# Summing a tile's scaled parts: a DMA that adds and one reduce, in place of GpSimd's adds and four VectorE adds

## The reference, cut to what matters

```
e = stack([tbl_0[ids[:, 0]], ..., tbl_39[ids[:, 39]]], axis=1)      # 512 x 40 x 16
x = x0 = e
for k in (k0, k1, k2):                                              # each 128 x H x 40
    x = einsum('bhd,bmd,ohm->bod', x, x0, k)
    outputs.append(sum(x, axis=-1))
z = concatenate(outputs, axis=1)                                    # 512 x 384
h = relu(concatenate([z, dense_ctx], 1) @ W_top1 + b_top1)
y = relu(h @ W_top2 + b_top2) @ W_top3
```

## Time and profile before

| | |
|---|---|
| median of 3 runs | 821.02 us |
| the profiled execution: span, first to last instruction | 817.8 us (the fastest of the three runs took 817.72) |
| TensorE busy | 690.5 us (84%) |
| VectorE busy | 668.2 us (82%) |
| ScalarE busy | 523.9 us (64%) |
| GpSimd busy | 499.1 us (61%) |
| mean granted TensorE clock | 0.971 |
| DMA moved | 43.07 MB, mean 53 GB/s |

### The profile page before, as it was taken

One profiled execution on the slowest core, in us unless ns is written; L12 is line 12 of the kernel. 1 busy time (PEld: TensorE's weight loads), 2 busy tenths in 40 slices (PEclk: granted clock), 3 DMA queues, 4 the chain that ended last, 5 costly groups with the idle time before them and its releaser, 6 DMA issues.

```text
span 817.8 us, 12851 instructions
## 1 busy us (share of the span) xinstructions
PE 690.5 (84%) x2558; PEld 477.1 (58%) x2558; DVE 668.2 (82%) x1542; ACT 523.9 (64%) x1753; POOL 499.1 (61%) x443
## 2 busy tenths in 40 slices
PE   0157988899898979797988898988979797998998
PEld 0126666566565757575655666665657575775384
DVE  2325989898988989898979898989979797989191
ACT  2205676676775767676666776767757676788193
POOL 6304767767667777685867767776767783564000
PEclk9998999999999999999999999999999998998599
DMA  6261111111212121212111111112121211010000
GB/s 187 63 171 61 44 55 53 45 64 38 70 25 76 22 77 25 76 31 69 35 60 46 49 58 45 62 37 70 19 77 22 75 30 64 36 42 26 0 1 1
DMA packets 45543, 43.07 MB, mean 53 GB/s; under 512 B 25615, under 2 KB 28943, under 8 KB 45216
## 3 DMA queue, kind: packets, MB, share of 16 engines
q1 hardware_dynamic: 40352, 41.07, 15.3%
q0 software_dynamic: 5120, 1.32, 2.2%
HBM read 41.06 MB, written 1.97 MB: 53 GB/s over the span
## 4 chain that ended last, share of the span: by engine, by line
DMA 37%; PE 21%; POOL 15%; issue 10%; SPq 7%; DVE 7%; ACT 2%; DVEq 1%; POOLq 0%; ACTq 0%
DMA pairs<-scratch 24%; POOL fold L350 7%; POOL x0g L309 7%; DMA scratch<-x0g 5%; DMA x0g<-in_table,rows_now 4%; DMA scratch<-scratch 4%; PE Y L622 4%; PE Y L624 3%; PE Y L623 3%; DVE chain L534 3%; SPq L268 3%; SPq L278 2%; DVE chain L497 2%; SPq L273 1%; DVE pairs L462 1%
## 5 line engine op out<-in xcount | busy, mean ns | idle before, releaser
L417 ACT ACTIVATE scaled<-Y,xtok 128x128 f32<-128x128 f32 x1536 | 422.7, 380 | 110.8 <-PE Y L624 100.5
L622 PE MATMUL Y<-k1lo,x1hi 128*128 128x512 f32 x640 | 296.5, 463 | 47.8 <-DVE chain L534 46.2
L624 PE MATMUL Y<-k1hi,x1lo 128*128 128x512 f32 x640 | 255.9, 400 | 0.0
L623 PE MATMUL Y<-k1hi,x1hi 128*128 128x512 f32 x640 | 255.4, 399 | 0.0
L534 DVE SCALAR_TENSOR_TENSOR chain<-Y,xtok,chain 128x128 f32<-128x128 f32 x768 | 211.6, 338 | 4.9 <-PE Y L624 4.8
L309 POOL DMA_INDIRECT x0g<-in_table,rows_now x160 | 174.5, 1091 | 42.1 <-issue 36.0
L350 POOL TENSOR_TENSOR fold<-fold,scaled 128x512 f32<-128x512 f32 x128 | 170.8, 1334 | 37.3 <-ACT scaled L417 28.3
L622 PEld LDWEIGHTS Y<-k1lo,x1hi 128*128 128x128 f32 x640 | 122.2, 191 | 118.3 <-DVE chain L534 77.6
L350 POOL TENSOR_TENSOR fold<-scaled 128x512 f32<-128x512 f32 x64 | 91.9, 1437 | 138.3 <-ACT scaled L417 111.1
L462 DVE TENSOR_TENSOR pairs<-pairs,A 120x512 f32<-120x512 f32 x112 | 96.9, 865 | 76.8 <-DMA pairs<-scratch 76.7
L623 PEld LDWEIGHTS Y<-k1hi,x1hi 128*128 128x128 f32 x640 | 122.7, 192 | 38.7 <-issue 14.4
(11 more groups left out here) (77 smaller groups left out, 453.4 us busy)
## 6 DMA issues: line engine op xcount, KB each, us to landing
pairs<-scratch SPq DMA_DIRECT2D x112, 240.0 KB
A<-scratch SPq DMA_DIRECT2D x16, 240.0 KB
k1raw<-in_k SPq DMA_DIRECT2D x1, 2560.0 KB, 10.5
x0g<-in_table,rows_now POOLq DMA_INDIRECT x160
k2s<-in_k SPq DMA_DIRECT2D x1, 2560.0 KB, 17.8
scratch<-x0g SPq DMA_DIRECT2D x64, 20.0 KB
pairs<-in_w SPq DMA_DIRECT2D x3, 256.0 KB
scratch<-scratch SPq DMA_DIRECT2D x16, 40.0 KB
```

The costliest lines, as they stand in the source:

```text
L417: ins = nc.scalar.activation(scaled[:, rank(c) - 1, i * O:(i + 1) * O], Y[(NCH * tile + c) % YB][:, i * O:(i + 1) * O], ACT.Copy, scale=xt ...
L622: nc.tensor.matmul(y, hi[:, tok], k1lo[:, cols], start=True, stop=False)
L623: nc.tensor.matmul(y, hi[:, tok], k1hi[:, cols], start=False, stop=False)
L624: nc.tensor.matmul(y, lo[:, tok], k1hi[:, cols], start=False, stop=True).then_inc(s_y, 1)
```

## The change

GpSimd's three adds a tile go. ScalarE now writes its six ranks into two buffers, each double: `sums` (four banks of 512: bank 0 is rank 1 and `chain`, banks 1, 2 and 3 are ranks 2, 3 and 6) and `more` (two banks: ranks 4 and 5). When rank 5 (chunk 6) is there, GpSimd first makes `diag`, then issues one DMA a tile that adds `more` (128 partitions x 4096 B) onto banks 1 and 2 of `sums`, and then the gathers. VectorE's four merge steps become one `tensor_reduce` over the sixteen 128-wide parts of `sums`, at c = 3 of the next tile; it waits for the DMA.

```diff
+ADDED = 2
+PARTS = NA - ADDED
-MERGE_AT = (0, 3, 3, 3)
+MERGE_AT = 3
...
                     pool.wait_ge(s_xtok, u * GPB + slot + 1)
                     pool.wait_ge(s_G, T + 1)
+                    pool.wait_ge(s_yA, NA * (T + 1) + NA - 1)
                     nc.gpsimd.tensor_tensor(diag[tile % 2][:, 0:M, :], ...)
-                    sums = fold[tile % 2]
-                    pool.wait_ge(s_merge, MERGE * T + 1)
-                    for a in range(2, NA - EXTRA):
-                        pool.wait_ge(s_yA, NA * (T + 1) + a + 1)
-                        if a > 2:
-                            pool.wait_ge(s_fold, FOLDS * (T + 1) + a - 2)
-                        nc.gpsimd.tensor_tensor(sums[:, :], scaled[:, 1, :] if a == 2 else sums[:, :],
-                                                scaled[:, a, :], ALU.add).then_inc(s_fold, 1)
+                    pool.dma_start(sums[tile % 2][:, BANK:BANK * (1 + ADDED)], more[tile % 2][:, :],
+                                   accum_op=ALU.add).then_inc(s_added[tile % 2], 16)
...
+            def place(par, r, i):
+                if r in (4, 5):
+                    return more[par][:, ((r - 4) * MB + i) * O:((r - 4) * MB + i + 1) * O]
+                k = (r - 1 if r < 4 else PARTS - 1) * MB + i
+                return sums[par][:, k * O:(k + 1) * O]
...
                             if rank(c) == 1:
-                                act.wait_ge(s_chain, STT * T + MB)
-                            elif rank(c) <= NA - EXTRA:
-                                act.wait_ge(s_fold, FOLDS * T + max(rank(c) - 2, 1))
-                            else:
-                                act.wait_ge(s_merge, MERGE * (T + 1) + rank(c) - NA + EXTRA)
+                                act.wait_ge(s_merge, T + 1)
+                            elif rank(c) == 4:
+                                act.wait_ge(s_added[tile % 2], 16 * (GPB * TPG // 2 * u + (tile + 2) // 2))
...
-            def merge(T, par, k):
-                ...
-                nc.vector.tensor_tensor(to, a, b, ALU.add).then_inc(s_merge, 1)
+            def merge(T, par, adds):
+                dve.wait_ge(s_chain, STT * (T + 2))
+                dve.wait_ge(s_added[par], 16 * adds)
+                dve.wait_ge(s_yA, NA * (T + 2))
+                nc.vector.tensor_reduce(x2[par][:, :], sums[par][:, :].rearrange("p (i o) -> p o i", o=O), AX.X,
+                                        ALU.add).then_inc(s_merge, 1)
```

More of the change, by code:

```diff
@@ L155, in build @@
         xtok = [sb(f"xtok{i}", [P, TPG, M]) for i in range(2)]
-        scaled = sb("scaled", [P, NA, BANK])
-        fold = [sb(f"fold{i}", [P, BANK]) for i in range(2)]
-        chain = [sb(f"chain{i}", [P, BANK]) for i in range(2)]
+        more = [sb(f"more{i}", [P, ADDED * BANK]) for i in range(2)]
+        sums = [sb(f"sums{i}", [P, PARTS * BANK]) for i in range(2)]
+        chain = [t[:, 0:BANK] for t in sums]
+        spot = sb("spot", [16, 8])
         x2 = [sb(f"x2_{i}", [P, O]) for i in range(2)]
@@ L183, in build @@
         w1cs, ctxs = A3[0][0:CTX, :], A3[1][0:CTX, :]
-        z2, w2s = pairs[3], over("fold0", "w2s", [P, H1 // P, H2])
-        h1 = scaled[:, 0:H1 // P, :]
+        z2, w2s = pairs[3], over("sums0", "w2s", [P, H1 // P, H2])
+        h1 = over("more0", "h1", [P, H1 // P, BANK])
         k2hi, k2lo = k1hi, k1lo
         Ghi = x1hi + pairs_hi[0:2]
-        Glo = x1lo + [pairs_hi[2], over("chain0", "Glo3", [P, B], f32r)]
+        Glo = x1lo + [pairs_hi[2], over("sums1", "Glo3", [P, B], f32r)]
         h2, ys = G[:, 0:2, 0:B], G[0:1, 2, 0:B]
@@ L217, in build @@
         s_chain = sem("chain_steps")
-        s_fold = sem("pool_folds")
+        s_added = [sem(f"added{i}") for i in range(2)]
         s_merge = sem("tile_sums_merged")
@@ L323, in _ @@
             pool.wait_ge(s_dones, 2)
-            nc.gpsimd.memset(fold[1][:, :], 0.0).then_inc(s_fold, FOLDS)
+            for i in range(2):
+                pool.dma_start(spot[:, 4 * i:4 * i + 4], ident_in[0:16, 0:4]).then_inc(s_added[i], 16)
             nc.gpsimd.memset(credit[:, 0:1], 0.0).then_inc(s_G, 1)
@@ L417, in body @@
                                 ins = nc.scalar.activation(
-                                    scaled[:, rank(c) - 1, i * O:(i + 1) * O],
+                                    place(tile % 2, rank(c), i),
                                     Y[(NCH * tile + c) % YB][:, i * O:(i + 1) * O], ACT.Copy,
@@ L478, in prep @@
                                             ALU.add).then_inc(s_x1free, 1)
-            def merge(T, par, k):
-                sums = chain[par]
-                if k == 0:
-                    dve.wait_ge(s_chain, STT * (T + 2))
-                else:
-                    dve.wait_ge(s_merge, MERGE * (T + 2) + k)
-                if k < EXTRA:
-                    dve.wait_ge(s_yA, NA * (T + 2) - EXTRA + k + 1)
-                    a, b, to = sums[:, :], scaled[:, NA - EXTRA + k, :], sums[:, :]
-                elif k == EXTRA:
-                    dve.wait_ge(s_fold, FOLDS * (T + 2))
-                    a, b, to = sums[:, :], fold[par][:, :], sums[:, :]
-                else:
-                    n = BANK >> (k - EXTRA)
-                    a, b = sums[:, 0:n], sums[:, n:2 * n]
-                    to = sums[:, 0:n] if k < MERGE - 1 else x2[par][:, :]
-                nc.vector.tensor_tensor(to, a, b, ALU.add).then_inc(s_merge, 1)
-            nc.vector.memset(chain[1][:, :], 0.0).then_inc(s_chain, STT)
-            nc.vector.memset(scaled[:, NA - EXTRA:, :], 0.0).then_inc(s_szero, 1)
-            nc.vector.memset(credit[:, 4:5], 0.0).then_inc(s_merge, MERGE)
+            def merge(T, par, adds):
[4 more added lines that the diff above has]
+                                        ALU.add).then_inc(s_merge, 1)
+            nc.vector.memset(chain[1], 0.0).then_inc(s_chain, STT)
+            nc.vector.memset(sums[1][:, BANK:], 0.0).then_inc(s_szero, 1)
+            nc.vector.memset(credit[:, 4:5], 0.0).then_inc(s_merge, 1)
             dve.wait_ge(s_w0, 32)
@@ L536, in body @@
                                     scalar=xtok[slot % 2][:, j, m:m + 1],
-                                    in1=chain[tile % 2][:, i * O:(i + 1) * O] if n >= MB else scaled[:, 0, i * O:(i + 1) * O],
+                                    in1=chain[tile % 2][:, i * O:(i + 1) * O],
                                     op0=ALU.mult, op1=ALU.add).then_inc(s_chain, 1)
@@ L540, in body @@
                             prep(step, u, slot)
-                        for k in range(MERGE):
-                            if c == MERGE_AT[k]:
-                                merge(T - 1, (tile - 1) % 2, k)
+                        if c == MERGE_AT:
+                            merge(T - 1, (tile - 1) % 2, GPB * TPG // 2 * u + (tile + 3) // 2)
             over_groups(dve, body)
-            for k in range(MERGE):
-                merge(NTILES - 1, (NTILES - 1) % 2, k)
-            dve.wait_ge(s_merge, MERGE * (NTILES + 2))
+            merge(NTILES - 1, (NTILES - 1) % 2, (NTILES + 3) // 2)
+            dve.wait_ge(s_merge, NTILES + 2)
             for c in range(NCH):
```

9 lines of the change are left out of this document (3 added, 6 removed).

## The result

| | before | after |
|---|---|---|
| median (lowest to highest), four runs each | 821.16 us (817.72 to 822.88) | 918.60 us (906.03 to 918.90) |
| profiled execution: span | 817.8 us | 916.8 us |
| mean granted TensorE clock | 0.971 | 0.916 |

The ratio is 1.126 with a 95% interval of 1.117 to 1.134: the changed kernel is 97 us slower. The forecast was 838 us, its range ended at 872; the sign was right and the size was not.

The account below looks back on a forecast made before the run. A loop of gathers, DMAs and work from product 0 to chunk 6 bounds the kernel. 3.0 - 2.3 = 0.7 us a slot gives +10, plus 3 and 4 at the end: 835 us profiled, 838 us forecast, range 790 to 872.

Parts of the forecast that it names:

- The adding DMA: GpSimd's queue: it delays the loads for products 0 and 1, 3.0 us a slot, taken between 2.0 and 5.4.
- the reduce: VectorE's merge: one reduce takes 2.28 us a tile in place of four steps of 3408 ns.
- the saving: VectorE from product 0 to chunk 6: cheaper merges and products save 2.3 us a slot as the mean.
- the prediction's own rule: Slot loop: savings count only from product 0 to chunk 6 of tile 2 or on GpSimd; DMA additions count in full.
- where 2.0 were counted: GpSimd from chunk 6 to the gathers: mask product and adding DMA's issue take 2.0 us and a wait, no net change.
- the second by some half: Loads before products 0 and 1: tile 3's adding DMA delays them in full, tile 0's by some half.
- lands late and every merge waits: Rival on the two-tile merge loop: with landing at 8 us, 46.2 us a slot, 876 us; chance 0.12.
- threshold of 6.8 us: Two-tile loop in slots with preparation: it passes the period from a landing of 6.8 us behind the issue.
- Slow reduce: Rival on VectorE's merge: the strided reduce takes 3.6 us, +1 us a slot, 856 us; chance 0.15.
- late landing: Rival on the adding DMA: it lands at 8 us and every merge waits, 876 us; chance 0.12.
- the contention of the forecast: Main case: the adding DMA delays the critical loads by 3.0 us a slot; 838 us, own range 822 to 854, chance 0.45.
- The last slot and the end: Last slot: two-tile loop of 8.6 us a tile against 7.56, +3 us; the final sum comes +3.8 us later.

Follow-up runs that it names:

- b2: Kernel before, with A and each rolled copy loaded by three DMAs of 40 partitions instead of one of 120: 759.8 us, ratio 0.922.
- b1: Kernel before, with the last two halvings of the merge replaced by one reduce over four parts: 815.7 us, ratio 0.996.
- e1: Changed kernel, with the reduce reading neighbours in memory instead of elements 512 B apart (it sums other elements): 891.6 us, ratio 1.089.
- e2: Changed kernel, with the adding DMA cut to 4 of 1024 columns, same issue and waits: 831.7 us, ratio 1.016.
- e6: Changed kernel, with both the reduce reading neighbours and the adding DMA cut to 4 columns: 803.6 us, ratio 0.979.
- e4: Changed kernel, with A and each rolled copy loaded by three DMAs of 40 partitions instead of one of 120: 785.5 us, ratio 0.957.
- e3: Changed kernel, with a plain copy of the same bytes in place of the adding DMA: 867.9 us, ratio 1.060.
- b3: Kernel before, with loads in three DMAs of 40 partitions and the last two halvings as one four-part reduce: 736.8 us, ratio 0.899.
- e7: Changed kernel, with loads in three DMAs of 40 partitions and four halving adds in place of the reduce: 770.0 us, ratio 0.940.

## Why the prediction was wrong

Three terms of the slot's sum were mis-sized. The adding DMA was put at 3.0 us and cost 5.4; the reduce was put at 2.28 us where it takes 3.74, 1.5 us a slot; the saving was put at 2.3 and was 1.1. That makes 2.4 + 1.5 + 1.2 = 5.1 us a slot, the difference between the 0.7 that were forecast and the 5.80 that came, 77 of the 82 us by which the span was off.

**What bounds the kernel.** Right: the loop of gather, DMAs and product 0, with its two halves. b2 and b1 show it from both sides: bringing the loads faster gave 61 us, while 49 us less of VectorE's work gave 5. By the prediction's own rule (a saving in the half from product 0 to the gather counts) b1 should have gained more than that: its half is 23.54 us against 23.50. Why is open; its granted clock in the loop is 0.94 against 0.98.

**The merges.** The step that took 2.28 us for the reduce, "by the reduce that is shown", failed. The shown reduce read neighbours; e1, which does so too, takes 2281 ns, as predicted, and the real one 3735. The hop of 512 B at every element costs 1.45 / 2048 = 0.7 ns an element. The Trainium skill (Vector Engine (DVE) Microarchitecture Reference, Measured stream behaviour on trn2) gives 1.73 ns an element where one source hops 4 KiB at every element, by which an estimated 3.6 us; the hop here is 512 B and the row, at 1.8 ns an element, agrees. The slow end was put into a rival at 0.15 while the sum took the other.

**GpSimd.** Right: the mask product (733 ns) and the issue (944 ns) are 1.7 us where 2.0 were counted, and in e2, which has both, the half from gather to product 0 is as before.

**What the saving is worth.** 2.3 us a slot were counted in the half from product 0 to the gather; e6 has 1.1, of which 0.85 in that half (22.65 us against 23.50). Where the other 1.2 is stays open. e6 waits 108.5 us for the copies instead of 76.7, so VectorE is there earlier without the copies being so, as in b1; and its granted clock in the loop is 0.94 against 0.98.

**The adding DMA.** The mechanism was right: three engines, 2.73 us on each (predicted 2.7 for two reads), collisions with the loads of product 0 and 1. Tile 1's, with the later copies, was left out. The term was mis-sized. 3.0 us a slot were taken, between 2.0 and 5.4; after less e2 is 49.47 - 44.49 = 4.98, and e1 less e6 47.99 - 42.59 = 5.40. The prediction counted what the DMA does to the loads, with "the second by some half", and took its own landing at 4.0 us behind the end of the issue. The profile counts from the issue's start, 0.94 us earlier: 7.9 us in the median is 7.0 on that scale, and the 4.5 of the last slot, where nothing is in its way, 3.6. So the landing alone was sized well, and what the loads do to it was not counted: its last part waits on those same three engines, as the slot above shows. That is the rival "lands late and every merge waits". Its threshold of 6.8 us was worked out with a reduce of 2.28 us; with 3.74 it is 5.3, and tiles 0 and 1 pass either.

**The rivals.** The failing step here is the way in which they were used. Slow reduce (+1 us a slot), late landing (+2.5 us a slot) and the contention of the forecast were given as alternatives with 0.15, 0.12 and 0.45, and the range ended 4 us below the dearest of them alone (876). They exclude each other in nothing. By the slots of the runs: -1.1 for what the change saves, +5.4 for the DMA's weight, +1.5 for the stride, 5.8 in all, times 15 is 87 (the three are steps from before over e6 and e1 to after, so they add up by construction). With the forecast's own upper ends, -2.3 + 5.4 + 1.0, a slot would have been 4.1 us longer, and the span 817.8 + 62 + 7 for the ends + 3.3 for the slow reduce in them, 890 us: outside the range that was given, and still 27 short, since the saving was smaller and the stride dearer than these ends.

**The last slot and the end.** Forecast +3 and +4, measured +11.7. The last tiles of the changed kernel, VectorE:

```profile
828.54 3.79 DVE L487 TENSOR_REDUCE x<-sums 128x128 f32<-128x2048 f32 x1 [0.33 <-DVE sums L525]
...
837.58 3.78 DVE L487 TENSOR_REDUCE x<-sums 128x128 f32<-128x2048 f32 x1
...
846.33 3.59 DVE L487 TENSOR_REDUCE x<-sums 128x128 f32<-128x2048 f32 x1 [1.76 <-issue]
```

From sum to sum it is 9.04 and 8.75 us where 8.6 were worked out and 7.56 stood before; at the middle reduce VectorE does not wait for the DMA, and TensorE's G waits for the reduce (1.19 us at 832.4). By the same reckoning (last x1lo to the end of the last sum, 48.3 us) e2 has 42.1 us, e6 37.4, before 36.6: 6.2 of the 11.7 for the DMA's weight, 4.7 for the stride, 0.8 for the rest. Without the stride 7.0 are left, which is what was forecast.

**What would show it.** Two signs pointed at the two rivals: a reduce above 3.6 us (slow reduce), and a landing over 5 us with VectorE waiting for it in the slots with preparation (late landing). The products came at 0.69 us as said, and in the slot shown product 0 starts 10.4 us behind the issue of its copy (said: a copy of 10 to 12 us). The interval of 44 to 45 us did not come, and ScalarE has no wait at rank 4 in the trace. VectorE at 35.2 of 45 us (said: about 35) is luck: the loop of both kernels, with the same columns as above, is

```profile
59.50:801.60 742.10, 610.62 (x2232) 435.93 (x2232) 582.53 (x1193) 449.81 (x1571) 257.01 (x271) 0.92 0.37 86
58.90:713.90 655.00, 579.00 (x2224) 411.23 (x2225) 587.02 (x1372) 447.49 (x1563) 454.63 (x390) 0.98 0.17 51
```

(after, then before). VectorE works 582.53 / 15 = 38.8 us a slot, where 35 of 45 in a slot of 44.4 meant 34.5; the slow reduce and the long slot cancel in the share.

**Left open.** The granted clock is 0.92 in the stretch shown (1.00 before), between the levels of 1.2 and 2.4 GHz, and the mean matmul of a chunk takes 476, 415 and 413 ns against 463, 399 and 400. TensorE idles more there ahead of it. By the two rows above its busy time for the same work is 610.62 / 15 = 40.7 us a slot against 38.6, so up to 2.1 of the 5.80 us can be the lower clock; in e4, whose loop has 0.97, it is 38.5 again. The lower clock would then be a part of what the waits cost and not a cause beside them, since it goes with the DMA's weight (e2: 39.1). How much of the 2.0 us by which the half from product 0 to the gather has grown is this, and how much the late sums, no run here separates. e2 and e3, at 0.953 and 0.937 for the whole execution, have 24.1 and 25.1 us for that half.

## What to carry to other kernels

Ask of a DMA that is to take work off an engine on which DMA engines it runs and who else is on them: here the changed kernel lost not by the instructions, which were issued for nearly nothing, but by 2.7 us on three engines that the critical loads used, in both directions. Before that, look at how many engines the critical loads have (share of 16 while they stream): a load on three of them was the kernel's real bound, and the same bytes by three DMAs of 40 partitions were worth more than either rewriting. And costs that don't exclude each other belong in one sum with its upper ends, not in separate rivals.

## What the runs showed of the hardware that was not expected

- An accumulating DMA of 128 x 4 KB costs its engines 2.73 us each, a plain copy of the same bytes 1.38; its issue takes GpSimd 944 ns (mean) against 597, and it lands at best 4.5 us behind the issue's start against 2.9.
- A `tensor_reduce` with a hop at each element isn't lengthened by GpSimd's adds as VectorE's own adds are: in b1 and b3 it takes 1083 ns on average and at most 1114, where in the earlier trace rows an add of 128 took 1.29 us beside GpSimd and 0.29 alone, and one of 256 takes 760 on average in the earlier trace rows and 452 in e7, which has no GpSimd adds.
- Three smaller DMAs were faster than one large one: 9.7 engines against 3.06, though SP issues 24 instead of 8 a group.
- While the adding DMA had 97.8% of the 16 engines, from 409 to 412 us, no packet of the loads in SyncE's queue moved, though the first of them had been issued at 408.62.
- The same layers behind the last sum took 57.7 us at a granted clock of 0.97 and 67.2 at 0.83.
